# Local attention values in 128x32 tiles: each half of 64 queries split into two groups of 32

## The reference, cut to what matters

```python
Kw = jnp.concatenate([Kp[:, :, :-1], Kp[:, :, 1:]], axis=3)
Vw = jnp.concatenate([Vp[:, :, :-1], Vp[:, :, 1:]], axis=3)
...
sc = jnp.einsum('bhnid,bhnjd->bhnij', Qb, Kw) / np.sqrt(D).astype(np.float32)
sc = jnp.where(mask[None, None], sc, -jnp.inf)
p = jax.nn.softmax(sc, axis=-1)
out = jnp.einsum('bhnij,bhnjd->bhnid', p, Vw)
```

## Time and profile before

| | us |
|---|---|
| time, median of 3 runs (lowest to highest) | 2784.46 (2783.8 to 2791.09) |
| the profiled execution, its own time | 2778.41 |
| its span, first to last instruction | 2776.6 |
| PE busy (weight loads) | 2597.7 (1766.3) |
| DVE / ACT / POOL busy | 1737.3 / 1199.2 / 966.5 |
| attention loop | about 57 to 1676 |
| choice of the first expert's tokens | about 1676 to 1799 |
| experts | about 1799 to 2777 |

### The profile page before, as it was taken

The page is one execution under the profiler, slowest core; times in us unless marked ns, Lnnn a source line. Parts: engine busy times, 40 slices in busy tenths (PEclk is TensorE's granted clock), DMA queues, the critical chain, the costliest instruction groups (busy, mean ns, idle before and its releaser), DMA issues. The chain is left out here.

```text
span 2776.6 us, 97280 instructions
## 1 busy us (share of the span) xinstructions
PE 2597.7 (94%) x41512; PEld 1766.3 (64%) x41512; DVE 1737.3 (63%) x5575; ACT 1199.2 (43%) x2659; POOL 966.5 (35%) x1417
## 2 busy tenths in 40 slices
PE   5999999999999999999999983399999999999998
PEld 3666666666766666666666662266666666666665
DVE  5666666666666666666666656775756667575600
ACT  2444445545444544444444430243333444433342
POOL 4332333433423333334233200134434343444333
PEclk9999999999999999999999995699999999999999
DMA  2110111101101111011010001012121121112020
GB/s 77 24 26 24 28 26 26 26 26 26 26 24 28 26 26 25 25 26 28 24 26 26 24 17 39 16 33 67 34 71 49 50 70 36 66 35 71 27 71 29
DMA packets 62599, 98.67 MB, mean 36 GB/s; under 512 B 13676, under 2 KB 47544, under 8 KB 62168
## 3 DMA queue, kind: packets, MB, share of 16 engines
q0 software_dynamic: 18624, 51.14, 6.9%
q1 hardware_dynamic: 43544, 41.29, 4.5%
HBM read 55.88 MB, written 33.82 MB: 32 GB/s over the span
## 5 line engine op out<-in xcount | busy, mean ns | idle before, releaser
L911 PE MATMUL banks<-hT,w 128*128 128x512 f32 x1024 | 469.8, 606 | 11.2 <-ACT hT L728 10.8
L1180 DVE TENSOR_REDUCE mx<-banks 128x8 f32<-128x1024 f32 x256 | 301.2, 1219 | 128.2 <-PE banks L1022 128.2
L702 ACT ACTIVATE probT<-banks 128x1024 f32<-128x1024 f32 x256 | 259.2, 1026 | 224.8 <-PE banks L1066 224.8
L739 ACT ACTIVATE hid<-banks,b 128x512 f32<-128x512 f32 x256 | 175.8, 687 | 400.9 <-PE banks L911 400.9
L911 PEld LDWEIGHTS banks<-hT,w 128*128 128x128 f32 x1024 | 188.0, 192 | 214.4 <-issue 198.5
L550 POOL TENSOR_TENSOR h<-ve,mhalf 128x2 f32<-128x2 f32 x128 | 92.0, 719 | 648.8 <-DVE ve L1221 648.7
L528 POOL DMA_INDIRECT rows<-in_tok_table,idx_now x132 | 138.4, 1049 | 399.9 <-DVE hres L1158 347.8
L1079 PEld LDWEIGHTS V_ps<-Ve,probT 128*64 128x64 f32 x4096 | 251.6, 139 | 34.6 <-issue 34.6
L1079 PE MATMUL V_ps<-Ve,probT 128*64 128x17 f32 x4096 | 264.4, 212 | 0.1
L1079 PE MATMUL V_ps<-Vo,probT 128*64 128x17 f32 x4096 | 264.4, 212 | 0.0
L593 POOL TENSOR_TENSOR orow<-orow,b 128x256 f32<-128x256 f32 x128 | 134.7, 1052 | 370.7 <-DVE orow L1345 369.6
(11 more groups left out here) (225 smaller groups left out, 5402.7 us busy)
## 6 DMA issues: line engine op xcount, KB each, us to landing
h_rows<-h SPq DMA_DIRECT2D x128, 130.0 KB, 2.0
w<-in_w SPq DMA_DIRECT2D x16, 1024.0 KB, 5.2
Qt<-low SPq DMA_DIRECT2D x512, 2.0 KB
Gq<-lowl SPq DMA_DIRECT2D x256, 2.0 KB
Kt<-units SPq DMA_DIRECT2D x256, 4.0 KB
rows<-in_tok_table,idx_now POOLq DMA_INDIRECT x132, 3.7
out_rows<-orow,idx_cur POOLq DMA_INDIRECT x128, 2.4
Gk<-units SPq DMA_DIRECT2D x64, 1.0 KB
```

The source lines that it names most:

```text
L702: nc.scalar.activation(dst[:, 2 * pair:2 * pair + 2, :], banks[:, 2 * pair:2 * pair + 2, :], ACT.Exp).then_inc(s_exp, 1)
L739: nc.scalar.activation(hid[:, m, :], S_ps[m % 2][:, 0:GT * P], ACT.Gelu_apprx_tanh, bias=b1[:, m:m + 1]).then_inc(s_hid, 1)
L911: mm = nc.tensor.matmul(S_ps[m % 2][:, 0:GT * P], w1[:, c, m * P:(m + 1) * P], hT[g % 2][:, c, :], start=c == 0, stop=c == KC - 1)
L1180: nc.vector.tensor_reduce(tops.rearrange("p (g h) -> p g h", g=2), banks[:, 2 * pair:2 * pair + 2, :].rearrange("p g (h k) -> p g h k", h= ...
```

## The change

Each of the 32 matmuls of line 1079 is replaced by two. Each takes 32 of the 64 stationary columns and writes 32 PSUM partitions, so that the four quarters of the 128 queries go to four column groups of the array, of 32 columns each. The moving operands, the columns of `V_ps`, the waits and the signal stay. The latent heads' matmuls stay at 64 columns.

```diff
@@ -1076,9 +1076,10 @@
                     for g in range(G):
                         h = 8 * c + 2 * g + j
                         for a, vals in ((0, Ve[par]), (1, Vo[par])):
-                            nc.tensor.matmul(V_ps[side[a], h * OW:(h + 1) * OW],
-                                             probT[t % 2][:, g, n * P + a * W:n * P + (a + 1) * W],
-                                             vals[:, t, h, :], start=True, stop=True)
+                            for at_ in range(a * W, (a + 1) * W, 32):
+                                nc.tensor.matmul(V_ps[at_:at_ + 32, h * OW:(h + 1) * OW],
+                                                 probT[t % 2][:, g, n * P + at_:n * P + at_ + 32],
+                                                 vals[:, t, h, :], start=True, stop=True)
                 for g in range(G):
                     at_ = (H + 2 * g) * OW
                     for a in range(2):
```

## The result

The change made the kernel slower: 2882.98 us (median, 2878.38 to 2885.84) against 2784.13 for the kernel before, a ratio of 1.0351 [1.0326, 1.0376]. The forecast was 2744 us, with a range of 2728 to 2800.

The account below looks back on a forecast made before the run. TensorE bounds the loop, with weight loads setting line 1079's pace; 0.73 us saved less 0.10 for the switch gives 0.63 per VAL, times 2 VALs and 32 sequences 40 us: 2744 us, range 2728 to 2800.

Parts of the forecast that it names:

- Instruction fetch: PE's instruction stream: 16,384 more records cost nothing; 10 us if some 60 added packets each stalled 0.16 us.
- the forecast's own burst: Line 1079's changed burst of 64 fp32 matmuls: taken as 1.10 us instead of 1.83, ends 1.01 and 1.70.
- the forecast's worst case: Instruction stream: each of some 60 added packets shows a stall of 0.16 us, 10 us in all.
- Feeding: Instructions reaching PE in the changed burst: 0.017 us per fp32 matmul, so 64 want 1.07 us.
- The "stall" of 0.16 us: Key scores, 1003.55 to 1003.72: read as PE stalling, to explain their slower pace of 0.0265 us per matmul.
- which VAL has room behind it: Line 1079's bursts: 0.63 us saved behind VAL 2 and VAL 3, nothing behind VAL 0 and VAL 1; 40 us.
- Rival 1: Line 1079's burst: only two column groups load at a time, burst 2.02 us, total 2811 us; chance 0.18.
- rival 4: Line 1079's burst: a whole-engine floor of 0.029 us per start doubles it, total 3029 us; chance 0.02.
- MX 3 and MX 4 do follow DVE: Line 797's transposes behind VAL 0 and VAL 1 already wait for DVE's maxima, following by 0.14 to 0.15 us.
- The switch from 32-wide to 64-wide tiles: From line 1079 to line 1085: changing tiling drains the engine, costing 0.10 us per VAL, bounds 0 and 0.10.
- The granted clock: PE in the attention loop: a sign of the forecast was that its clock would still be 1.00.
- Rival 2: Line 1079's burst runs with holes at the key scores' pace, 1.70 us, total 2782 us, no change; chance 0.12.

Follow-up runs that it names:

- the stretch: Kernel before plus 1024 fp32 matmuls in 32-column groups (128x32 tiles) in one row ahead of the loop: 2836.8 us.
- val23: Kernel before with the 32-column split in only the line 1079 bursts VAL 2 and VAL 3 of each sequence: 2830.39 us, ratio 1.0164.
- val01: Kernel before with the 32-column split in only the line 1079 bursts VAL 0 and VAL 1 of each sequence: 2838.35 us, ratio 1.0199.
- bf16_2: Kernel before (64-wide tiles) with the local probabilities and values in bf16: 2726.95 us, ratio 0.9784.
- bf16_4: Changed kernel (32-wide tiles) with the local probabilities and values in bf16: 2739.6 us, ratio 0.9841.
- kt_late: Changed kernel with four of SP's DMAs into Kt held back until the burst VAL 1 is over: 2938.66 us, ratio 1.0553.
- stretch_f2: Kernel before plus 512 fp32 matmuls in its own 128x64 tiles, two column groups, ahead of the loop: 2833.9 us.

## Why the prediction was wrong

*The step that failed is "Instruction fetch".* It had the right cause in hand, 16,384 more records on the instruction stream, and costed it at nothing, 10 us at most. The reason given, queue 8 at 0.8% of the DMA engines' time and a DMA share of 0.10, asks whether there is bandwidth. It should have asked how long one packet takes to follow another, and how many records PE wants meanwhile. Both were in reach: the earlier trace rows give 5.41 MB in 330 packets, in the DMA records of the kernel before no two of them start less than 3.3 us apart, and the forecast's own burst wanted 256 records in 1.1 us. What the runs showed in its place: packets no closer than 3.2 us, 3.7 on average in the stretch, and 116.1 us of gaps that end when one has come. That is 1.8 us for each of the 64 added packets, where the forecast's worst case took 0.16. A burst of before asks for 128 records in 1.83 us, 256 in 3.7, no faster than they come. The changed one asks for 256 in 1.06, with 32 of line 1085 and key scores of 192 behind it, and empties what is buffered.

*"Feeding" read a pace that holds only within what is buffered.* 0.017 us for one fp32 matmul was right for a burst without a hole, 1.06 us by loads and 1.09 by matmuls (forecast 1.10). As a lasting pace it is 0.056 in the stretch, three times as much. A short run of starts shows the engine's pace, not the supply's. The "stall" of 0.16 us beside it was misread: in the earlier trace rows rows are left out between 1003.55 and 1003.72, and four more loads start there, the first and the last of them these:

```profile
1003.56 0.13 PEld L1062 LDWEIGHTS banks<-Qt,Kt 32*64 32x64 f32 x1
...
1003.61 0.13 PEld L1060 LDWEIGHTS banks<-Qt,Kt 32*64 32x64 f32 x1
1003.72 0.13 PEld L1062 LDWEIGHTS banks<-Qt,Kt 32*64 32x64 f32 x1
```

The longest pause is 0.11 us, and matmuls go on starting in it.

*Where the holes fall, no dependency tells.* The forecast asked which VAL has room behind it. A hole comes where the buffered records end, and so it hits the key scores (+49.2 us) and line 1085 (+34.6) as well as the burst itself. `val23` and `val01` show it: half the records, about half the loss, whichever VALs they are in.

*What was right.* Rival 1 (two loads at a time) and rival 4 (a floor per start) are refuted: four groups start every 0.033 us together. (In rival 1, 32 x 0.064 is 2.05 and not 2.02; it should have read 2815.) MX 3 and MX 4 do follow DVE: the VAL 0 shown ends in 0.65 us of waiting, and `bf16_2` loses 89.8 us there. The switch from 32-wide to 64-wide tiles was forecast at 0.10 us in all. In the kernel after line 1086 follows the last start by 0.113 us (median) instead of 0.052, and its 16 starts take 0.436 instead of 0.415, so it is 0.08; in `bf16_4` the first of the two is 0.11, in `bf16_2`, without a switch, 0.03. The Trainium skill, "TensorEngine Tiling (Array Packing)", Key Properties, says that a change of the tiling mode drains the engine; these rows agree. The granted clock did not stay at 1.00: the 37.4 us at 0.50 may make up to 19 of the 99.9 us (half of them, an estimate), which no run parts from the holes.

*Rival 2 named the sight and not the cause.* "A burst with holes" is what the trace shows; but it was priced at the pace of the key scores, 1.70 us, and given no change. Such pauses as the key scores of before show, 0.11 us at the longest in the unit read, are not the 1.4 to 2 us of a missing packet. What makes them is not explained by these runs.

## What to carry to other kernels

Before a matmul is split into more and smaller ones, count the records that a burst and what follows it ask for, and hold it against the time in which the instruction stream has brought as many elsewhere in the same trace; the stream's share of the DMA bandwidth says nothing about it. Idle time put down to "issue" in a row of matmuls, at places that move from one sequence to the next, is the sign. What helped here were bf16 operands in the wider tile, fewer records and a shorter burst at once; and then the next wait has to be looked for.

## What the runs showed of the hardware

- PE's instructions came in packets of 16 KB. In a row of matmuls with nothing else, 256 records came every 3.5 to 4.3 us, whether in fp32 or bf16, and no two packets of that queue started less than 3.2 us apart in any trace. In the kernel after, each of 102 gaps over 0.5 us between PE's records ended 1.2 to 1.6 us after a packet had landed.
- While SP issues DMAs, PE's starts thin out for 0.1 to 0.4 us at a time, even if no packet is missing; without those issues VAL 1 was 0.6 us shorter. Pauses of 0.2 to 0.3 us also end 0.18 and 0.64 us after POOL's gather starts (`kt_late`), wherever in the burst it starts.
- In bf16 a 64-column start follows its own group's last after 0.030 us, in fp32 after 0.058.
- At the head of the kernel TensorE ran at half its pace, through the 55 us of matmuls without a pause in `stretch_f2` too, up to the first clock record of the trace (41.1 us in the kernel before, 95.2 in `stretch_f2`); ahead of that record a printed 1.00 tells nothing.
